# Four places for swapped halves, query sums ahead of the cosines, output weights behind each job's own work

## What is computed

```python
q = (layernorm(x) @ wq)      # 32 heads of 128
k = (ctx @ wk); v = (ctx @ wv)  # 8 heads of 128, each shared by 4 query heads
q, k = rope(q), rope(k)      # x * cos + rotate_half(x) * sin
attn = softmax(q @ k.T / sqrt(128) + mask)
x = x + tanh(g_xattn) * (attn @ v @ wo)
x = x + tanh(g_ffn) * routed_lora(layernorm(x))
```

## Time and profile before

| | us |
|---|---|
| median of 3 runs | 1166.37 (1165.32 to 1166.63) |
| the profiled execution | 1167.51 |
| its span, first to last instruction | 1165.7 |
| TensorE busy in it | 1116.2 |

### The profile page before, as it was taken

One profiled execution on the slowest core, in us unless ns is written; L12 is line 12 of the kernel. 1 busy time (PEld: TensorE's weight loads), 2 busy tenths in 40 slices (PEclk: granted clock), 3 DMA queues, 4 the chain that ended last, 5 costly groups with the idle time before them and its releaser, 6 DMA issues.

```text
span 1165.7 us, 17071 instructions
## 1 busy us (share of the span) xinstructions
PE 1116.2 (96%) x5664; PEld 921.9 (79%) x5664; DVE 930.1 (80%) x1413; ACT 632.1 (54%) x1090; POOL 560.9 (48%) x513
## 2 busy tenths in 40 slices
PE   7999999789999999999999999999999999999997
PEld 6788888667777777777778777888888888888775
DVE  7984756788878887888888878888888888888887
ACT  6462345556666666666665554555555555555441
POOL 4651468676666666666664323233333333333320
PEclk9999999999999999999999999999999999999999
DMA  6869963494555455555448815653535353532201
GB/s 224 280 233 368 299 207 136 145 347 169 177 171 175 170 177 167 179 165 182 158 174 339 295 46 183 198 180 100 171 100 180 129 200 119 177 118 91 73 1 73
DMA packets 93509, 206.26 MB, mean 177 GB/s; under 512 B 8816, under 2 KB 41712, under 8 KB 87536
## 3 DMA queue, kind: packets, MB, share of 16 engines
q1 hardware_dynamic: 93424, 205.18, 51.8%
HBM read 122.31 MB, written 82.84 MB: 176 GB/s over the span
## 4 chain that ended last, share of the span: by engine, by line
PE 49%; POOL 17%; DVE 14%; issue 13%; ACT 6%; DMA 1%; DVEq 0%; POOLq 0%; SPq 0%; ACTq 0%
PE attn L856 15%; PE proj L797 12%; PE attn L749 5%; POOL rot L1588 5%; PE score L814 4%; PE turned L749 3%; PE score L749 3%; DVE q_r L1043 3%; POOL wq_s L1563 2%; DVE p_low L1123 2%; ACT rot L1371 2%; POOL prob_odd L1595 1%; DVE acc L1143 1%; PE attn L841 1%; PE turned L825 1%
## 5 line engine op out<-in xcount | busy, mean ns | idle before, releaser
L856 PE MATMUL attn<-wo_s,o_s 128*128 128x512 f32 x1536 | 384.4, 399 | 11.6 <-DVE o_s L1131 11.6
L856 PEld LDWEIGHTS attn<-wo_s,o_s 128*128 128x128 f32 x1536 | 282.8, 189 | 80.2 <-DVE o_s L1131 23.5
L797 PE MATMUL proj<-xB,wq_s 128*128 128x512 f32 x1344 | 337.1, 394 | 7.6 <-DVE q_r L1085 6.3
L1588 POOL TENSOR_TENSOR rot<-rot,tab 128x512 f32<-128x512 f32 x160 | 218.8, 1369 | 214.4 <-ACT rot L1371 214.3
L797 PEld LDWEIGHTS proj<-xB,wq_s 128*128 128x128 f32 x1344 | 253.1, 189 | 62.1 <-DVE q_r L1085 7.1
L1048 DVE TENSOR_TENSOR q_r<-q_r,rot 128x512 f32<-128x512 f32 x128 | 115.3, 901 | 57.8 <-POOL rot L1588 48.2
L1043 DVE TENSOR_TENSOR q_r<-q_r,tab 128x512 f32<-128x512 f32 x128 | 153.7, 1201 | 2.0 <-ACT rot L1371 0.7
L1416 ACT ACTIVATE o_s<-attn 128x512 fp32r<-128x512 f32 x128 | 70.2, 596 | 118.6 <-PE attn L843 118.0
L814 PEld LDWEIGHTS score<-k_r,q_r 128*128 128x128 f32 x1024 | 125.6, 194 | 8.0 <-issue 2.7
L814 PE MATMUL score<-k_r,q_r 128*128 128x64 f32 x1024 | 123.1, 274 | 0.5 <-DVE prob_even L1105 0.3
L1143 DVE SCALAR_TENSOR_TENSOR acc<-attn,gates_t,acc 128x512 f32<-128x512 f32 x128 | 96.0, 750 | 33.2 <-PE attn L856 31.2
(11 more groups left out here) (180 smaller groups left out, 1472.4 us busy)
## 6 DMA issues: line engine op xcount, KB each, us to landing
wq_kept<-wq_s SPq DMA_DIRECT2D x16, 1792.0 KB, 6.5
wq_s<-wq_kept SPq DMA_DIRECT2D x16, 1792.0 KB, 8.6
v_kept<-vst SPq DMA_DIRECT2D x64, 256.0 KB, 4.6
v_s<-v_kept SPq DMA_DIRECT2D x128, 128.0 KB, 4.9
wo_kept<-wo_s SPq DMA_DIRECT2D x32, 512.0 KB, 2.9
wo_s<-wo_kept SPq DMA_DIRECT2D x32, 512.0 KB, 5.4
k_kept<-kst SPq DMA_DIRECT2D x32, 256.0 KB, 2.0
wq_raw<-in_wq SPq DMA_DIRECT2D x16, 512.0 KB, 7.5
```

The source lines that it names most:

```text
L797: last = e.matmul(dst[:, :], wq_s[:, b % 2, A, s, kt, :], xB[:, B, mv, kt, :], start=(first and kt == 0 and m == 0), stop=(kt == 1 and m = ...
L856: last = e.matmul(attn[bp][:, :], o_s[:, s, bp, h, :], wo_s[n % WO_SLOTS][:, m, :], start=(h == 0 and i == 0), stop=(h == GROUP - 1 and i ...
L1588: e.tensor_tensor(r3, r3, sin, ALU.mult).then_inc(times_sin, 1)
```

## The change

- `rot` gets four places from key job 48 to key job 59 and the query sums between (`FOUR`, r = 16 to 32). The two further ones are `x_third`, a buffer for rows of x that has been read for the last time by then. Later r go back to two places. Each shift waits for the last add that used its own place.
- `p_low` lies on the same memory as `x_third`, so its clearing moves from job 54 to job 62 on GpSimd, and waits for the last add of the four-place stretch.
- On VectorE the query sums beside a job stand ahead of that job's cosine, and no longer behind it.
- On ScalarE, from job 56 on, splits of `wq` and `wo` stand behind the job's own shift, copies and query shift, and no longer ahead of them; `wq` now comes before `wo`.
- On SyncE the refills of `raw` beside jobs 59 and 61 stand ahead of the store of the key block before.

```diff
-ZEROS_BESIDE = 54
+FOUR_UNTIL, ZEROS_BESIDE = 60, 62
...
+FOUR = range(ROPE_NO[JOBS[VALUES_MADE]], ROPE_NO[JOBS[FOUR_UNTIL]])
+ROT_SLOT = [(r - FOUR.start) % 4 if r in FOUR else r % 2 for r in range(len(ROPES))]
+ROT_BEFORE = [max([p for p in range(r) if ROT_SLOT[p] == ROT_SLOT[r]], default=None) for r in range(len(ROPES))]
...
         def rotated(r):
-            return rot[:, r % 2, :]
+            return rot[:, ROT_SLOT[r], :] if ROT_SLOT[r] < 2 else x_third[:, ROT_SLOT[r] - 2, :]
...
+                if n in (59, 61):
+                    fetch_raw(RAW + (n - 59) // 2)
                 if n:
                     store_job(JOBS[n - 1])
...
-                if n in (59, 61):
-                    fetch_raw(RAW + (n - 59) // 2)
...
+                for q in SUMS_BESIDE.get(n, ()):
+                    q_sum(*q)
                 finish_job(n)
...
-                for q in SUMS_BESIDE.get(n, ()):
-                    q_sum(*q)
...
             def shift(r, src):
                 half = DH // 2
-                if r >= 2:
-                    e.wait_ge(rope_added, r - 1)
+                if r == FOUR.start:
+                    e.wait_ge(x_turned, 4 * len(X_PAIRS))
+                if ROT_BEFORE[r] is not None:
+                    e.wait_ge(rope_added, ROT_BEFORE[r] + 1)
...
             for n in range(len(JOBS)):
-                for w in SPLITS_BESIDE.get(n, ()):
+                for w in SPLITS_BESIDE.get(n, ()) if n < KEYS_3_MADE else ():
                     raw_split(w)
-                for w in WQ_BESIDE.get(n, ()):
+                for w in WQ_BESIDE.get(n, ()) if n < KEYS_3_MADE else ():
                     wq_split(*w)
...
                 if n in ROPE_BESIDE:
                     q_shift(*ROPE_BESIDE[n])
+                for w in WQ_BESIDE.get(n, ()) if n >= KEYS_3_MADE else ():
+                    wq_split(*w)
+                for w in SPLITS_BESIDE.get(n, ()) if n >= KEYS_3_MADE else ():
+                    raw_split(w)
...
+                if n == ZEROS_BESIDE:
+                    e.wait_ge(rope_added, FOUR.stop)
+                    e.memset(p_low[:, :, :, :].bitcast(F32), 0.0).then_inc(zeros_set, 1)
                 if n == SCORES_AFTER:
                     subtract_max(0)
...
-                if n == ZEROS_BESIDE:
-                    e.wait_ge(x_turned, 4 * len(X_PAIRS))
-                    e.memset(p_low[:, :, :, :].bitcast(F32), 0.0).then_inc(zeros_set, 1)
```

## The result

The changed kernel takes 1162.9 us (median of 8 runs, 1159.65 to 1164.01) against 1166.36 (8 runs, 1164.36 to 1167.72) for the kernel before on the same chip: 0.9967 of the time, 95% interval 0.9956 to 0.9979, so 2.4 to 5.1 us faster. The forecast was 1162.0 with faster by over 0.2% as the likeliest case. The profiled execution of the changed kernel took 1160.38 us with a span of 1158.6; that of before 1167.51 and 1165.7.

What follows compares the result with a forecast made beforehand. TensorE, 96% busy, was taken to wait on a late output-weight row holding ScalarE, then on VectorE and GpSimd's shared line. Terms -5.5, +3.1 and -2.0 gave -4.4 us: 1166.37 to 1162.0 us, range 1157.0 to 1165.5.

Runs made afterwards that it cites:

- e6: The kernel before with one edit: query sums ahead of the job's cosine on VectorE; 1167.27 us (1 run).
- e12: The kernel before with only the four places and the query sums ahead of the job's cosine; 1164.5 us (1 run).
- e4: The changed kernel with SyncE's refills of raw behind the key store again; 1159.69 us (1 run).

## What to carry to other kernels

Remove waits in the order in which they bind: here one late row at the head of an in-order engine hid everything else, and edits that brought up to 2.0 us once it was gone brought nothing before. Two edits can also need each other: more places without early sums, or early sums without more places, were no better than neither. Undoing one of them at a time made each look worth 2.5 us. Where two engines share a line of work, look for its gaps as well as its work; more buffers are worth what they close of these gaps, and moving work that is ready into one gave the fastest complete kernel of the study, without another byte or instruction. And look for the fall of the clock at the place to which a wait moves, not only where it leaves; what it costs there depends on what else the next operation waits for (0.21 us in the changed kernel, 1.68 in e6 and e12).

## What the runs showed of the hardware

A VectorE operation on two SBUF inputs of 128x512 took 0.68 us alone and up to 1.8 beside a GpSimd operation, GpSimd's sine 1.27 alone and up to 1.8. Where both had work, they took turns, and who came 0.08 us first could decide a whole turn, as at 215.01 in the changed kernel.

TensorE's granted clock fell to its lower level behind idle times of about 2 to 3 us in some executions and not in others: the scores ran at it behind a wait of 2.11 us in the changed kernel (3.65 us) and not behind 2.08 in e4 (2.00). Eight runs of one kernel, at mean granted clocks of 0.991 to 0.995, lay 4 us apart, as much as the whole change. A difference of two single profiled spans (7.1 us here) was therefore nearly twice the effect.
